# The last pair's cross attention without products of zeros

## The reference, cut to what matters

```python
x = x + _L0_attn_ref(_layernorm(x, axis=-1), ...)             # 16 heads, 4 groups of keys
x = x + _L0_xattn_ref(_layernorm(x, axis=-1), ctx_1024, ...)  # 16 heads, 345 keys and 16 more
x = x + _L0_ffn_ref(_layernorm(x, axis=-1), ...)              # shared expert, top 4 of 60 experts
```

## Time and profile before

| | us |
|---|---|
| median of 3 runs | 1175.94 |
| the three runs | 1175.72, 1175.94, 1178.64 |
| the profiled execution, its own time | 1178.55 |
| its span, from the first to the last instruction | 1176.8 |
| mean granted clock of PE over the span | 0.977 |
| PE busy | 1087.5 (92% of the span) |
| DVE busy | 502.1 (43%) |
| ACT busy | 263.9 (22%) |
| POOL busy | 370.3 (31%) |

### The profile page before, as it was taken

How to read it: one execution, slowest core, us unless ns; L and a number is a source line. 1 busy time by engine, 2 the same in 40 slices (tenths; PEclk the granted TensorE clock), 3 DMA queues, 4 the chain that set the end, 5 groups by cost and what they waited for, 6 DMA issues and landing times.

```text
span 1176.8 us, 18687 instructions
## 1 busy us (share of the span) xinstructions
PE 1087.5 (92%) x5538; PEld 588.5 (50%) x5538; DVE 502.1 (43%) x1385; ACT 263.9 (22%) x806; POOL 370.3 (31%) x843
## 2 busy tenths in 40 slices
PE   3999799999899989999889999999999979899797
PEld 1444465445554456544655555555545535444454
DVE  7843674339654395543846701222122111111144
ACT  0332232414332243333414010111111111111000
POOL 3575451855527563374200370000000000000272
PEclk9999899999999999999999999999999999999899
DMA  8999201000010000102013986999999999999753
GB/s 319 345 397 383 92 2 57 15 1 13 2 56 15 13 1 9 47 15 96 2 48 102 367 319 237 384 349 379 366 383 380 372 378 368 380 361 369 252 140 110
DMA packets 76584, 233.11 MB, mean 198 GB/s; under 512 B 11362, under 2 KB 13766, under 8 KB 68814
## 3 DMA queue, kind: packets, MB, share of 16 engines
q1 hardware_dynamic: 58830, 197.90, 46.9%
q10 hardware_dynamic: 11520, 20.98, 5.1%
q0 software_dynamic: 6144, 13.13, 3.6%
HBM read 178.75 MB, written 53.22 MB: 197 GB/s over the span
## 4 chain that ended last, share of the span: by engine, by line
PE 62%; SPq 14%; DVE 11%; DMA 7%; issue 5%; ACT 1%; DVEq 0%; ACTq 0%
PE ps L852 13%; PE ps L941 7%; PE ps L1146 6%; SPq L474 6%; PE ps L1229 6%; PE ps L1330 5%; PE ps L1225 5%; SPq L547 4%; PE ps L1261 3%; DMA arena<-in_se_down 3%; PE ps L1257 2%; DMA arena<-in_w 2%; PE ps L998 2%; PE ps L1203 2%; DMA arena<-in_x 2%
## 5 line engine op out<-in xcount | busy, mean ns | idle before, releaser
L852 PE MATMUL ps<-arena 128*100 128x512 f32 (+3 forms) x552 | 208.3, 524 | 4.3 <-ACT arena L1352 3.6
L786 POOL DMA_INDIRECT arena<-ys_d,slot_u x32 | 36.5, 1141 | 415.7 <-issue 412.5
L852 PEld LDWEIGHTS ps<-arena 128*100 128x100 f32 (+1 forms) x552 | 83.1, 173 | 94.9 <-issue 86.5
L1229 PE MATMUL ps<-arena 128*64 128x352 f32 x640 | 107.9, 494 | 16.6 <-issue 12.6
L2084 DVE COPY arena<-ps 128x512 f32<-128x512 f32 x40 | 27.7, 692 | 222.1 <-PE ps L1217 222.1
L941 PE MATMUL ps<-arena 128*100 128x512 f32 x256 | 114.1, 593 | 0.0
L1146 PE MATMUL ps<-arena 128*128 128x400 f32 x288 | 98.3, 501 | 2.2 <-DVE arena L2064 1.1
L1225 PE MATMUL ps<-arena 128*128 128x352 f32 x320 | 98.1, 459 | 0.8 <-issue 0.8
L1404 ACT ACTIVATE arena<-ps,arena 100x345 f32<-100x345 f32 x128 | 69.6, 547 | 107.8 <-DVE arena L1851 105.3
L1229 PEld LDWEIGHTS ps<-arena 128*64 128x64 f32 x640 | 48.9, 147 | 70.7 <-issue 60.4
L712 POOL TENSOR_TENSOR arena<-arena 115x512 f32<-115x512 f32 (+1 forms) x29 | 30.5, 1051 | 160.9 <-DVE arena L1777 125.1
(11 more groups left out here) (229 smaller groups left out, 1524.6 us busy)
## 6 DMA issues: line engine op xcount, KB each, us to landing
arena<-in_w SPq DMA_DIRECT2D x60, 1408.0 KB, 17.6
arena<-in_w SPq DMA_DIRECT2D x60, 512.0 KB, 17.6
xs_d<-zero SPq DMA_DIRECT2D x5, 3328.0 KB, 25.2
arena<-in_w SPq DMA_DIRECT2D x60, 192.0 KB, 19.8
arena<-xs_d ACTq DMA_DIRECT2D x40, 256.0 KB, 8.0
ys_d<-arena ACTq DMA_DIRECT2D x40, 256.0 KB, 8.8
ys_d<-zero SPq DMA_DIRECT2D x2, 3328.0 KB, 25.6
arena<-in_se_up SPq DMA_DIRECT2D x11, 512.0 KB, 6.7
```

The costliest lines, as they stand in the source:

```text
L852: last = nc.tensor.matmul(ps[0:m, k, 0:cols[1] - cols[0]], lhs(c), w[:, c, cols[0]:cols[1]], start=(c == 0), stop=(c == n_c - 1))
L1229: last = nc.tensor.matmul(ps[half * HALF:(half + 1) * HALF, 3 + gu, 0:I], xsT[1][:, c, half * HALF:(half + 1) * HALF], w13_s[s][1 + half][ ...
```

## The change

`keep_busy` issues nothing in the last pair. The first three pairs keep their zero products, and so does `open_context` (line 1013), which opens the accumulation of a bank with one product of zeros. What the other engines do is the same.

```diff
                 def keep_busy(j, n):
 
-                    for _ in range(n):
+                    for _ in range(n if more else 0):
                         nc.tensor.matmul(ps[:, 6 + j, 0:2 * S], zero[:, 0:P], zero[:, 0:2 * S], start=False, stop=False)
```

## The result

The changed kernel took 1184.17 us (median of 8 runs, 1180.59 to 1189.86), the kernel before 1177.28 beside it (median of 8, 1172.75 to 1188.77). The ratio is 1.0069 with a 95% interval of 1.0043 to 1.0095: slower by 8.1 us (5.1 to 11.2), worked out on 1177.28. The two medians lie 6.9 apart, inside that interval. The profiled execution of the changed kernel has a time of its own of 1183.14 and a span of 1181.4, at a mean granted clock of 0.967 (0.977 before).

A forecast was written before the change was run, and what follows sets the result against it. PE and DVE take turns bounding the last pair; at the lower clock PE bounds steps 3 to 6. 9.1 + 1.7 - 2.0 = 8.8 us on 1178.55 gave 1187.35, lowered to 1186.0 towards the median; range 1177.0 to 1195.0.

The forecast's parts named there:

- Step 0, 0.70: Last pair, step 0: scores stand right behind the zeros, so removing these wins 0.70 us at the upper clock.
- Step 2, 0.3: Last pair, step 2: scores come sooner but DVE was idle only 0.31 us before them; 0.3 of 1.38 us won.
- Steps 3 to 6 at the lower clock, +9.1 of a range of 8.3 to 10.0: From 567.3 to 585.7 at clock 0.50: 8.3 us longer if PE's idle time is swallowed, 10.0 if kept; 9.1 taken.
- the 1.875: Ratio of PE time at clock 0.50 to 1.00 for scores, values and two transpose chunks: 4.50 against 2.40 us.
- The projection of step 6 starts low, +1.7: Projection at 585.7 begins at the lower clock and brings the upper one back: 3.61 us against 1.88, 1.7 more.
- Step 6, 0.70: Last pair, step 6: scores behind the zeros with nothing else late, 0.70 us won at the upper clock.
- Step 8, -0.3, and the end: Last pair, step 8: third chunk needs a bank that DVE's copy frees; 0.3 us won, 0.4 at most.
- the far rival: Clock stays at 0.50 to the pair's end: 590.3 to 602.6 takes 4.4 or 6.4 us more, 1191.75 to 1193.75; chance 0.08.
- The shift passes whole: A shift of the end of the attention pass goes whole into the kernel's time, as later transfers start when PE frees buffers.
- The step down of 1.35: From 1187.35 to 1186.0: half of the 2.6 us by which the runs' median lies below the profiled execution.
- the short falls: Rival, last pair: clock falls but returns at once, say three short stretches; +0.7 us, 1179.25, or 1177.95 at the median; chance 0.18.
- a held clock: Rival, last pair: clock holds and only the 2.7 us gain remains, 1175.85, outermost 1173.3; chance 0.16.

The follow-up runs named there:

- the kernel with 60 added products: 60 zero products added between the last pair and the shared expert's first products, against the kernel before; ratio 1.0162 (1.0114 to 1.0209).
- the added products: 20 or 60 zero products added between the last pair and the shared expert, each against the kernel before; ratios 1.0074 and 1.0162.

## Why the prediction came out right, step by step

The time was 1184.17 where 1186.0 was predicted, on the side and for the reason given: without the zeros the clock falls. But that the sum of +8.8 came so close is in part luck: the terms behind it were off and cancel. In the cuts of the table the prediction says -1.0 up to step 3, +10.1 from there to step 7 (9.1 and 1.7, less 0.7) and -0.3 behind it. Measured, in the three profiles against the first of the kernel before: -1.9, then +3.2, +6.9 and +7.1, then +5.3, +4.9 and +5.1.

*Step 0, 0.70.* Right: the scores of step 1 start 0.71 sooner after those of step 0 in all three profiles (4.94 for 5.65).

*Step 2, 0.3.* Too small: from the scores of step 2 to those of step 3 it takes 5.67 us for 6.89 (6.61 and 6.75 in the other two profiles of the kernel before). In the kernel before, the fall at 563.9 caught the zeros there (1.38 on the chain for four records, where the same count took 0.70 elsewhere). In the profile of the kernel with 60 added products, where the clock stays up in this piece and the pair's zeros are all there, it takes 5.77. So at the upper clock the zeros of step 2 cost 0.1, and with the fall 0.8 to 1.1 more.

*Steps 3 to 6 at the lower clock, +9.1 of a range of 8.3 to 10.0.* The mechanism was right, the size was off. From step 3 to step 7 in the longer two profiles 6.9 and 7.1 are lost, and with step 6's 0.70 given back 7.6 and 7.8, below the low end. PE swallowed most of its idle time, the assumption of the 8.3: in the third profile it idles 1.04 of 27.30 us. Between the values of step 3 and the projection of step 6, the kernel before (all engines, then line 1018 alone, for which the columns of DVE, ACT and POOL are left out) and the third profile of the changed kernel:

```profile
567.52:585.65 18.13, 16.39 (x214) 13.06 (x211) 15.10 (x48) 10.61 (x34) 1.71 (x4) 1.00 0.00 1
567.52:585.65 18.13, 2.93 (x14) 2.26 (x14) 1.00 0.00 1
566.68:592.46 25.78, 25.20 (x201) 19.26 (x197) 16.17 (x50) 11.05 (x35) 2.46 (x8) 0.51 0.00 1
```

PE's own work is 16.39 - 2.93 = 13.46 us before and 25.20 after, a ratio of 1.87: the 1.875 was right. Mis-sized were mainly the zeros, 2.93 us on PE where 2.44 had been read off the chain; the own work was 13.5 us and not 14.2, and the loss of this piece is 7.65. And in the first profile the clock rose after 17.0 us already, at 582.3, and only 3.2 are lost.

*The projection of step 6 starts low, +1.7.* This failed. It takes 3.60 us at 1.00 in every profile. My reason was that a projection brings the clock back, read from the first pair; in the last pair the clock was up before the projection began, in all three. What does bring it back was not found out.

*Step 6, 0.70.* Right where the clock is up: in the first profile steps 6 to 7 take 7.09 for 7.80.

*Step 8, -0.3, and the end.* This failed most. I kept the upper clock from the projection on, and gave the second fall 0.08, as the far rival. The fall is there in every profile, from about 600 to 613. The loss of 4.9 to 5.3 looks like what that rival had priced (4.4 to 6.4), but it is made up otherwise. The rival priced only the piece up to the last projections, all of it at the lower clock. That piece, from the scores of step 7, takes 15.07, 15.31 and 15.30 us for 12.32, only 2.7 to 3.0 more, since the clock falls only 5.8 to 6.7 us behind the scores. The other 1.9 to 2.6 come from the last projections, which the rival left out: line 852's 16 records there take 6.94, 6.34 and 6.46 us, where they took 4.38. That the rival's figure fits is luck. Its place was wrong too: it was to come on top of a full 9.1 and 1.7.

*The shift passes whole.* Right within what the timed runs can tell (the added products); some 2 us taken back can't be ruled out.

*The step down of 1.35* to the median of the runs: the profiled execution of before lies 1178.55 - 1177.28 = 1.27 above the median of its 8 runs, which fits. But this offset belongs to one execution: that of the changed kernel lies 1.03 below its median, so the fit is luck.

*The range.* The lower bound of 1177.0 was called the low end of the short falls, for which the prediction's own sum gives 1177.95.

Of the signs that were named, in the first profile of the changed kernel, the clock at 0.50 held for 17 of the 24 us between 564 and 588; the scores of steps 4, 5 and 6 started 6.9, 6.5 and 6.8 us after those ahead of them, a little under the 7 that I gave; VectorE's busy share fell from 15.17 of 18.40 us to 13.13 of 17.00; and the shared expert started 7.8 us later. The rivals of a held clock and of short falls are ruled out for this kernel by the two long stretches. The rule of the Trainium skill in "TensorE: Matmul & The Clock Gate", section "HAM oscillation — how this bites in real kernels", would have kept the clock up. The trace differs from the rule.

In this case the clock fell behind waits of 0.83 us, twice, in step 2, and stayed down with PE 96% busy (26.26 of 27.30 us). Nor do these waits decide alone: the kernel with 60 added products has the same two waits of 0.83 us in step 2, with zeros and scores behind them, and its clock doesn't fall. What sets the moment of a fall stays open.

## What to carry to other kernels

Before you take filler work out of PE's list, look for what its clock does where that filler is already absent: the first pair's start and the short fall at 563.9 told here that the clock can fall and stay down, which the profile of the stretch itself could not, though not what brings it back. Price each piece up to the next stage with a bound of its own, not only the piece that comes first to mind, because a clock that falls once without the filler can fall again wherever it is missing. And read PE's busy share only beside its granted clock: in the slow stretch of the slower kernel PE was the busier (16.17 of 17.00 us, for 16.66 of 18.40). Where two sums agree, look at what each of them is made of: the rival's 4.4 to 6.4 us fitted a loss that came in part from another place.

## What the runs showed that was not expected

- With products of 32 columns of weights the clock stayed up as with those of 128 (ratio 0.9999), and both take 333 ns.
- One program has low stretches of different lengths from one execution to the next, 17.0 and 27.3 us at the same place, 3.4 and 3.7 us apart in the measure; why is open.
- The short fall near 564 comes and goes: it is there in all three profiles of the kernel before and absent in that of the kernel with 60 added products, whose pair has the same code, and in that of the kernel with zeros in steps 0 to 5, which is the same up to there; with it step 2 took 6.6 to 6.9 us, without it 5.8.
- A stretch at 0.50 went on for 27.3 us while PE was busy 26.26 of them, with scores, values, transposes and the products for the 16 keys.
